# Top-32 cross-attention in a four-layer network: who normalises the first groups, where the keys are made, and where the statistics stand

## The chip, the cores and the metric

The kernel runs on one core of a Trainium2 chip. The core has a TensorE (PE) for matrix products, a VectorE (DVE), a ScalarE (ACT) and a GpSimd (POOL) for elementwise work, and a SyncE (SP) that issues DMAs. The engines run their own instruction streams and wait for each other by semaphores. The metric is the device time of one execution in microseconds.

## What is computed

The network has four layers, each a cross-attention and a feed-forward part, on x of 32 x 128 x 128 (batch, token, feature) in float32. The part that matters here is the attention of layer 1. Its scores keep only the 32 largest of 128 in each row, and its result sets a scale and a shift ("film") on a normalised x:

```
Q = (x_text @ Wq).reshape(Bb, Tt, H, DH)
K = (x_vision @ Wk).reshape(Bb, Gg, H, DH)
scores = jnp.einsum('bthd,bghd->bhtg', Q, K) / np.sqrt(DH).astype(np.float32)
topv, topi = jax.lax.top_k(scores, K_TOP)
probs = jax.nn.softmax(topv, axis=-1)
attn = jnp.zeros_like(scores).at[bi, hi, ti, topi].set(probs)
attn_mean = attn.mean(axis=1)
c_t = jnp.einsum('btg,bgd->btd', attn_mean, V)
x = layernorm(x_text, g_norm_in, b_norm_in)
scale_in, shift_in = jnp.split(c_t @ W_film_in + b_film_in, 2, axis=-1)
x = x * (1.0 + mod_gate * scale_in) + mod_gate * shift_in
y = s4d(x, log_dt, A_re, A_im, C_re, C_im, D_skip)
```

H is 4, DH 32, K_TOP 32. x_text is itself the layernorm of the running x, so x is normalised twice.

## The kernel before

The program is a row of stages with a barrier of all engines between them: stage_front (layer 0 and preparations), stage_film, stage_mix, stage_attention16, stage_fp8, stage_moe, store. stage_film consists of film_in, which is changed, and convolve, which is not. X lies in SBUF as k.X for the whole program.

film_in treats 32 samples i, one a 128 x 128 tile. Four samples are a group g (8 groups), two are a pair (16 pairs). Every engine runs one written-out loop over a pass number p from -5 to 18, and the source order within the loop is the order of its queue. Nothing reorders it. In pass p:

- DVE (from L1408): the statistics of group (p+5)/2 in odd p (group_stats L97: four BN_STATS; group_moments L178 to L188: seven small instructions), the second rstd of group (p+3)/2 in odd p (three small instructions, L1422 to L1427), then four rounds for pair p. A round is 8 MAX8 (L1441, the 8 largest of 128 in each row, 4 heads of 2 samples) and 8 MATCH_REPLACE8 (L1447, takes them out). After four rounds the 32 largest are gone from c_left.
- POOL: c_shift of pair p (L1251, minus the largest, a bias of the exp); in even p rstd of group (p+4)/2 by a pow (L1257) and its normalisation into c_xn (L1262, four instructions); in even p the second rstd and the scaled copy of group (p+2)/2 (L1271 to L1279, three instructions of 128 x 512); the shares of pair p-1 (L1283 to L1293); the film of pair p-2 (L1299, L1301).
- PE: transposes of the weights of pair p-2 (L1315), the scores of pair p+1 (L1325, L1328), in odd p the transposes of c_xn of group (p+3)/2 (L1336), in even p the key product K (L1342, from k.cT, which is there from the start) and the query product Q (L1344) of group (p+2)/2, then for pair p-2 the products L1349 and L1353.
- ACT: exp of what is left of pair p-1 (L1366, c_exb), exp of the scores of pair p (L1373, c_exa), copies of scores (L1380, c_sc), in odd p of c_xnT (L1386), in even p of c_kT (L1392) and c_qT (L1394), then c_wT (L1397), c_aT (L1400) and c_fo (L1406). The difference of the two exps is the softmax over the 32 largest.

A pass is called odd or even by its p. Groups 3 to 7 have their transposes in passes 3, 5, 7, 9 and 11 and K and Q in passes 4, 6, 8, 10 and 12. Rows of q, k and xT share two banks of PSUM: K writes bank 7, the transposes and Q write bank 6.

Of the kernel before, what the change touches and what calls it, by code (L numbers as in the profile page):

```python
# [16 lines left out]
G = 4  # L17
W = G * S
# [1145 lines left out]
def film_in(nc, w, ps, k):  # L1164
# [6 lines left out]
    PAIRS, GROUPS = B // 2, B // G  # L1171
    FIRST, LAST = -5, PAIRS + 3
    TAKES = 2 * H * ROUNDS
    with ExitStack() as ctx:
        def tmp(name, shape, dt=F32):
            return ctx.enter_context(nc.sbuf_tensor("c_" + name, shape, dt))
# [36 lines left out]
        def pair(p):  # L1213
            return (2 * p, 2 * p + 1) if 0 <= p < PAIRS else ()
# [19 lines left out]
        def _(pool):  # L1234
# [10 lines left out]
            for p in range(FIRST, LAST):  # L1245
                for i in pair(p):

                    pool.wait_ge(top_done, TAKES * p + H * (i % 2 + 1))
                    if i >= 4:
                        pool.wait_ge(exb_done, H * (i - 3))  # L1250
                    pool.tensor_scalar(shift[:, i % 4, :], first[:, i % 2, :, 0], -SCALE, None,  # L1251
                                       ALU.mult).then_inc(shift_done, 1)
                if (p + 4) % 2 == 0 and 0 <= (p + 4) // 2 < GROUPS:
                    g = (p + 4) // 2
                    u = g % 2
                    pool.wait_ge(ve, g + 1)
                    pool.tensor_tensor(nm.rstd[:, u], nm.ve[:, u], k.half[:, 0:G], ALU.pow).then_inc(rstd, 1)  # L1257
                    pool.wait_ge(rstd, g + 1)
                    if g >= 4:
                        pool.wait_ge(x3_done, G * (g - 3))  # L1260
                    for j in range(G):
                        pool.tensor_scalar(xn[:, g % 4, j, :], k.X[:, G * g + j, :], nm.mean[:, u, j:j + 1],  # L1262
                                           nm.rstd[:, u, j:j + 1], ALU.subtract, ALU.mult).then_inc(xn_done, 1)
                    pool.tensor_copy(k.mean1[:, G * g:G * g + G], nm.mean[:, u]).then_inc(kept, 1)
                    pool.tensor_copy(k.rstd1[:, G * g:G * g + G], nm.rstd[:, u]).then_inc(kept, 1)
                if (p + 2) % 2 == 0 and 0 <= (p + 2) // 2 < GROUPS:
                    g = (p + 2) // 2
                    u = g % 2
                    x2 = xn[:, g % 4]
                    pool.wait_ge(ve2, g + 1)  # L1270
                    pool.tensor_tensor(rstd2[:, u], rstd2[:, u], k.half[:, 0:G], ALU.pow).then_inc(rstd2_done, 1)  # L1271
                    pool.wait_ge(rstd2_done, g + 1)
                    pool.wait_ge(xT_ps, g + 1)
                    pool.tensor_tensor(x2, x2, rstd2[:, u].rearrange("p (j o) -> p j o", o=1)
                                       .broadcast_to([128, G, 128]), ALU.mult).then_inc(x2a, 1)
                    pool.wait_ge(x2a, g + 1)
                    pool.tensor_tensor(x2, x2, rows(k.gin1), ALU.mult).then_inc(x2b, 1)
                    pool.wait_ge(x2b, g + 1)
                    pool.tensor_tensor(x2, x2, rows(k.bin1), ALU.add).then_inc(x2c, 1)  # L1279
                for i in pair(p - 1):  # L1280
                    a = i % 2
                    pool.wait_ge(exb_done, H * (i + 1))
                    pool.tensor_tensor(share[:, a, :], tota[:, i % 4, :], totb[:, a, :],  # L1283
                                       ALU.subtract).then_inc(tot_done, 1)
                    pool.tensor_tensor(exa[:, i % 4], exa[:, i % 4], exb[:, a], ALU.subtract).then_inc(diff_done, 1)
                    pool.wait_ge(tot_done, i + 1)
                    pool.tensor_tensor(share[:, a, :], share[:, a, :], minus[:], ALU.pow).then_inc(inv_done, 1)
                    pool.wait_ge(inv_done, i + 1)
                    pool.tensor_tensor(share[:, a, :], share[:, a, :], tshare[:, i:i + 1].broadcast_to([128, H]),
                                       ALU.mult).then_inc(share_done, 1)  # L1290
                    pool.wait_ge(share_done, i + 1)
                    pool.wait_ge(diff_done, i + 1)
                    pool.tensor_tensor(exa[:, i % 4], exa[:, i % 4], share[:, a, :].rearrange("p (h o) -> p h o", o=1)  # L1293
                                       .broadcast_to([128, H, 128]), ALU.mult).then_inc(part_done, 1)
                for i in pair(p - 2):
                    x2, f = xn[:, (i // G) % 4, i % G, :], fo[:, i % 2, :]
                    pool.wait_ge(fo_done, i + 1)
                    pool.wait_ge(x2c, i // G + 1)
                    pool.tensor_tensor(x2, x2, f[:, 0:128], ALU.mult).then_inc(filmed, 1)  # L1299
                    pool.wait_ge(filmed, i + 1)  # L1300
                    pool.tensor_tensor(k.x3[:, :, i:i + 1], x2.rearrange("p (c o) -> p c o", o=1),  # L1301
                                       f[:, 128:256].rearrange("p (c o) -> p c o", o=1), ALU.add).then_inc(x3_done, 1)

        @block.tensor
        def _(pe):
            pe.wait_ge(consts, 3)
            pe.wait_ge(zero_aT, 1)
            for p in range(FIRST, LAST):
# [20 lines left out]
                    m.then_inc(sc_ps, 1)  # L1329
                if (p + 3) % 2 == 0 and 0 <= (p + 3) // 2 < GROUPS:  # L1330
                    g = (p + 3) // 2
                    pe.wait_ge(xn_done, G * (g + 1))
                    if g:
                        pe.wait_ge(qT_done, g)
                    for j in range(G):
                        m = pe.transpose(ps[:, 6, j * S:j * S + S], xn[:, g % 4, j, :], k.ident[:])  # L1336
                    m.then_inc(xT_ps, 1)
                if (p + 2) % 2 == 0 and 0 <= (p + 2) // 2 < GROUPS:
                    g = (p + 2) // 2
                    if g:  # L1340
                        pe.wait_ge(kT_done, g)
                    pe.matmul(ps[:, 7, :], k.wk1[:], k.cT[:, W * g:W * g + W], start=True, stop=True).then_inc(k_ps, 1)  # L1342
                    pe.wait_ge(xT_done, g + 1)
                    pe.matmul(ps[:, 6, :], k.wq1[:], xnT[:], start=True, stop=True).then_inc(q_ps, 1)  # L1344
                for i in pair(p - 2):
# [10 lines left out]
        def _(act):  # L1356
            act.wait_ge(consts, 3)
            act.wait_ge(zero_aT, 1)
            for p in range(FIRST, LAST):
# [20 lines left out]
                    act.activation(sc[:, i % 4], ps[:, 0:H, 0:128], ACT.Identity).then_inc(sc_done, 1)  # L1380
                if (p + 3) % 2 == 0 and 0 <= (p + 3) // 2 < GROUPS:
                    g = (p + 3) // 2
                    act.wait_ge(xT_ps, g + 1)
                    if g:
                        act.wait_ge(q_ps, g)
                    act.activation(xnT[:], ps[:, 6, :], ACT.Identity).then_inc(xT_done, 1)  # L1386
                if (p + 2) % 2 == 0 and 0 <= (p + 2) // 2 < GROUPS:
                    g = (p + 2) // 2
                    if g >= 2:
                        act.wait_ge(sc_ps, G * (g - 1))  # L1390
                    act.wait_ge(k_ps, g + 1)
                    act.activation(kT[:, g % 2, :], ps[:, 7, :], ACT.Identity).then_inc(kT_done, 1)  # L1392
                    act.wait_ge(q_ps, g + 1)
                    act.activation(qT[:, g % 2, :], ps[:, 6, :], ACT.Identity).then_inc(qT_done, 1)  # L1394
                for i in pair(p - 2):
# [11 lines left out]

        @block.vector  # L1408
        def _(dve):
            for p in range(FIRST, LAST):  # L1410
                if (p + 5) % 2 == 0 and 0 <= (p + 5) // 2 < GROUPS:
                    g = (p + 5) // 2
                    if g >= 2:
                        dve.wait_ge(kept, 2 * (g - 1))
                        dve.wait_ge(rstd2_done, g - 1)
                    group_stats(dve, nm, norm, g % 2, lambda u, j: k.X[:, G * g + j, :])
                    group_moments(dve, nm, norm, g // 2, g % 2)
                if (p + 3) % 2 == 0 and 0 <= (p + 3) // 2 < GROUPS:
                    g = (p + 3) // 2
                    u = g % 2  # L1420
                    dve.wait_ge(rstd, g + 1)
                    dve.tensor_tensor(rstd2[:, u], nm.rstd[:, u], nm.rstd[:, u], ALU.mult).then_inc(rr, 1)  # L1422
                    dve.wait_ge(rr, g + 1)
                    dve.scalar_tensor_tensor(out=rstd2[:, u], in0=nm.ve[:, u], scalar=EPS, in1=rstd2[:, u],
                                             op0=ALU.subtract, op1=ALU.mult).then_inc(vr, 1)
                    dve.wait_ge(vr, g + 1)
                    dve.tensor_scalar(rstd2[:, u], rstd2[:, u], EPS, None, ALU.add).then_inc(ve2, 1)  # L1427
                for r in range(ROUNDS if pair(p) else 0):
                    done = TAKES * p + 2 * H * r
                    for i in pair(p):  # L1430
                        a = i % 2
# [1467 lines left out]
```

## Time and profile before

| | us |
|---|---|
| median of 3 runs | 1556.45 (1553.75 to 1558.42) |
| profiled execution, time | 1556.44 |
| profiled execution, span | 1554.5 |
| film_in within the span | 218 to 505 |

The span runs from the first to the last recorded instruction. Busy time over the span: PE 77%, DVE 65%, ACT 44%, POOL 38%. These are means over stages of different kinds; in film_in DVE is busy for nearly all the time, and at the end of the program PE is. A row of the timeline gives the start of an instruction or of several alike, its length, engine, line, output and inputs, and in brackets how long its engine had been idle and who released it. L12 is line 12 of the kernel before.

### The profile page before, as it was taken

Reading aid. Unit: us, or ns where it says so; the run is one execution under the profiler, and the core shown is the slowest. Engines: PE = TensorE matmul, PEld = TensorE weight load, DVE = VectorE, ACT = ScalarE, POOL = GpSimd, SP = SyncE. Lnnn points to the kernel's source line nnn. Section 1 sums busy time; section 2 is a strip of 40 time slices with the busy share of each in tenths; the row PEclk is TensorE's granted clock in tenths of the full one; section 3 lists DMA queues with packets and bytes.
Section 4 is the critical chain, followed back from the end, with each engine's and each line's share of the span. In section 5 each row is a group of like instructions: output and inputs, shape, how many; then the busy total and the mean of one; then the engine's idle time right before and its main releaser. Section 6 shows DMA issues by size and latency. Waiting matters only on the chain. (4 is left out here: it accounts for less than half of the span.)

```text
span 1554.5 us, 30934 instructions
## 1 busy us (share of the span) xinstructions
PE 1201.6 (77%) x10597; PEld 813.4 (52%) x10597; DVE 1010.5 (65%) x3921; ACT 685.5 (44%) x1990; POOL 585.7 (38%) x792
## 2 busy tenths in 40 slices
PE   3676743676666678884799897489999969999997
PEld 3443322343443445553577676146666647777765
DVE  6876649999994379852577776557766544444432
ACT  3343335556565344320344443146666633433332
POOL 3466665888876155421222321223333310000000
PEclk8588865666667789996899999589999979898988
DMA  6310041000000511000000000000000000000001
GB/s 164 83 41 1 0 106 26 15 18 28 25 22 28 150 41 42 15 14 14 2 3 3 3 3 3 1 1 1 2 1 2 1 1 1 0 0 0 0 0 54
DMA packets 63678, 35.54 MB, mean 23 GB/s; under 512 B 23925, under 2 KB 61424, under 8 KB 63538
## 3 DMA queue, kind: packets, MB, share of 16 engines
q1 hardware_dynamic: 62234, 33.45, 8.0%
q8 instruction: 76, 1.25, 0.3%
q14 instruction: 64, 0.52, 0.1%
q10 hardware_dynamic: 1304, 0.33, 0.1%
HBM read 25.21 MB, written 6.42 MB: 20 GB/s over the span
## 5 line engine op out<-in xcount | busy, mean ns | idle before, releaser
L2774 DVE SCALAR_TENSOR_TENSOR k_X<-ps,m_gt,k_X 128x128 f32 (+1 forms) x256 | 72.1, 344 | 125.4 <-PE ps L2673 125.4
L2703 ACT ACTIVATE m_hid<-ps,k_b 128x512 f32<-128x512 f32 x128 | 81.8, 684 | 137.5 <-PE ps L2673 127.7
L2673 PEld LDWEIGHTS ps<-k_w,m_hid 128*128 128x128 f32 x1024 | 123.1, 192 | 26.8 <-issue 17.2
L2664 PE MATMUL ps<-m_xnT,k_w 128*128 128x512 f32 x256 | 130.5, 641 | 1.1 <-DVE m_lg L2719 1.1
L2673 PE MATMUL ps<-k_w,m_hid 128*128 128x128 f32 x1024 | 123.4, 275 | 0.0
L2380 POOL TENSOR_TENSOR l_p<-l_p,l_rsum 128x512 f32<-128x512 f32 x64 | 65.2, 1039 | 152.5 <-DVE l_rsum L2611 152.5
L2182 DVE TENSOR_REDUCE g_top<-ps 128x8 f32<-128x1024 f32 x64 | 75.4, 1220 | 50.5 <-PE ps L2050 50.5
L1447 DVE MATCH_REPLACE8 c_left<-c_top,c_left 128x128 f32<-128x128 f32 x384 | 100.9, 276 | 0.0
L2492 ACT ACTIVATE l_p<-ps,l_shift 128x128 f32<-128x128 f32 x256 | 91.3, 387 | 20.2 <-DVE l_shift L2549 20.2
L2130 ACT ACTIVATE g_pT<-ps 128x1024 f32<-128x1024 f32 x64 | 62.0, 1021 | 85.4 <-PE ps L2066 85.4
L692 PE MATMUL ps<-f_expT,f_xeT 128*128 128x512 f32 x128 | 71.0, 686 | 33.6 <-DVE k_X L1064 33.6
L1325 PE MATMUL ps<-c_kT,c_qT 32*128 32x128 f32 x256 | 22.3, 429 | 74.4 <-ACT c_sc L1380 73.1
L1441 DVE MAX8 c_top<-c_left 128x8 f32<-128x128 f32 x384 | 78.6, 277 | 0.0
L121 POOL TENSOR_TENSOR m_rstd<-m_ve,k_half 128x8 f32<-128x8 f32 x4 | 6.6, 1638 | 185.9 <-DVE m_ve L114 185.9
L822 ACT ACTIVATE f_part<-ps,f_wf 128x128 f32<-128x128 f32 x128 | 36.5, 369 | 89.4 <-issue 66.2
L2664 PEld LDWEIGHTS ps<-m_xnT,k_w 128*128 128x128 f32 x256 | 48.6, 208 | 42.6 <-issue 41.1
L692 PEld LDWEIGHTS ps<-f_expT,f_xeT 128*128 128x128 f32 x128 | 25.2, 219 | 67.2 <-DVE k_X L1064 47.9
L1064 DVE SCALAR_TENSOR_TENSOR k_X<-ps,f_wf,k_X 128x128 f32<-128x128 f32 x128 | 44.5, 350 | 24.0 <-PE ps L692 20.6
L1315 PEld LDWEIGHTS ps<-k_ident,c_exa 128*128 128x128 f32 x256 | 45.6, 266 | 25.5 <-POOL c_exa L1293 13.1
L1325 PEld LDWEIGHTS ps<-c_kT,c_qT 32*128 32x128 f32 x256 | 14.5, 260 | 83.8 <-issue 78.2
L2492 ACT ACTIVATION_READ_ACCUMULATOR l_p<-ps,l_shift 128x1 f32 x256 | 58.3, 228 | 0.0
L1353 PE MATMUL ps<-k_wfilm,c_aT 97*128 97x512 f32 x64 | 54.0, 991 | 0.4
(515 smaller groups left out, 3250.2 us busy)
## 6 DMA issues: line engine op xcount, KB each, us to landing
v_toep<-kpad SPq DMA_DIRECT2D x4, 1024.0 KB, 10.4
fo_dram<-c_fo SPq DMA_DIRECT2D x32, 128.0 KB, 1.7
v_late<-kpad SPq DMA_DIRECT2D x4, 1024.0 KB, 10.5
d_fo<-fo_dram SPq DMA_DIRECT2D x8, 512.0 KB, 3.5
k_X<-in_x SPq DMA_DIRECT2D x8, 256.0 KB, 3.5
out<-k_X SPq DMA_DIRECT2D x4, 512.0 KB, 5.4
f_cx<-in_ctx SPq DMA_DIRECT2D x4, 384.0 KB, 5.3
c_cx<-in_ctx SPq DMA_DIRECT2D x4, 384.0 KB, 3.6
```

The lines of the kernel that those rows point to most:

```text
L692: pe.matmul(ps[:, 4 + (2 * b + h) % 3, :], xeT[:, t % 2, u, cols], expT[:, 4 * h:4 * h + 4, :].rearrange("p e d -> p (e d)"), start=True, ...
L1353: pe.matmul(ps[:, 4 + a, :], aT[:, a, :], k.wfilm[:], start=True, stop=True).then_inc(film_ps, 1)
L1441: dve.max((first if r == 0 else top)[:, a, h, :], (sc if r == 0 else left)[:, i % 4, h, :]).then_inc(top_done, 1)
L1447: dve.match_replace(left[:, i % 4, h, :], (first if r == 0 else top)[:, a, h, :], (sc if r == 0 else left)[:, i % 4, h, :], TAKEN).then_in ...
L2130: act.activation(pT[:, n % 2, 2 * h:2 * h + 2, :].rearrange("p a n -> p (a n)"), ps[:, 4 + 2 * h:6 + 2 * h, :].rearrange("p a n -> p (a n) ...
L2182: dve.tensor_reduce(top[:, (n + 1) % 2, :].rearrange("p (r c) -> p r c", r=R)[:, 2 * h:2 * h + 2, 0:R], ps[:, 2 * h:2 * h + 2, :].rearrang ...
L2380: pool.tensor_tensor(p[:, n % 3, 4 * a:4 * a + 4, :], p[:, n % 3, 4 * a:4 * a + 4, :], rsum[:, n % 3, 4 * a:4 * a + 4].rearrange("p (h o) ...
L2492: act.activation(p[:, i % 3, h, :], ps[:, 2 * (i % 2) + a, 128 * b:128 * b + 128], ACT.Exp, bias=shift[:, i % 2, h:h + 1], scale=SCALE, ac ...
L2664: pe.matmul(ps[:, 4 * u + q, :], k.w1_3[:, e, 128 * q:128 * q + 128], xnT[:, u], start=True, stop=True).then_inc(s["hid_ps"].sem, 1)
L2673: m = pe.matmul(ps[:, 4 * u + 2 + e % 2, j * S:j * S + S], hid[:, u, q, j * S:j * S + S], k.w2_3[:, e, q, :], start=q == 0, stop=q == 1)
L2703: act.activation(hid[:, u, q, :], ps[:, 4 * u + q, :], ACT.Gelu, bias=k.b1_3[:, 2 * e + q:2 * e + q + 1]).then_inc(s["hid"].sem, 1)
L2774: dve.scalar_tensor_tensor(out=xj[u][j], in0=ps[:, 4 * u + 2 + e % 2, j * S:j * S + S], scalar=gt[:, u, j, e:e + 1], in1=xj[u][j], op0=ALU ...
```

## The change

DVE's loop is rewritten. It begins with the statistics of groups 0 and 1, then normalises both into c_xn itself (apply), each followed by its second rstd (second). POOL leaves these eight instructions out. Then it loops over the pairs only: the statistics of the next group (moments) stand behind the first round of pair 0 and of odd pairs, the second rstd of group 2 behind the third round of pair 0, and that of later groups ahead of an odd pair. PE makes K in odd passes, ahead of the transposes, in place of even passes ahead of Q, and ACT copies c_kT there, ahead of c_xnT.

```diff
+    EARLY_GROUPS = 2
@@ gpsimd
-                    for j in range(G):
+                    for j in range(G if g >= EARLY_GROUPS else 0):
                         pool.tensor_scalar(xn[:, g % 4, j, :], k.X[:, G * g + j, :], nm.mean[:, u, j:j + 1],
                                            nm.rstd[:, u, j:j + 1], ALU.subtract, ALU.mult).then_inc(xn_done, 1)
@@ tensor
                 if (p + 3) % 2 == 0 and 0 <= (p + 3) // 2 < GROUPS:
                     g = (p + 3) // 2
+                    if g:
+                        pe.wait_ge(kT_done, g)
+                    pe.matmul(ps[:, 7, :], k.wk1[:], k.cT[:, W * g:W * g + W], start=True, stop=True).then_inc(k_ps, 1)
                     pe.wait_ge(xn_done, G * (g + 1))
...
                 if (p + 2) % 2 == 0 and 0 <= (p + 2) // 2 < GROUPS:
                     g = (p + 2) // 2
-                    if g:
-                        pe.wait_ge(kT_done, g)
-                    pe.matmul(ps[:, 7, :], k.wk1[:], k.cT[:, W * g:W * g + W], start=True, stop=True).then_inc(k_ps, 1)
@@ scalar
                     g = (p + 3) // 2
+                    if g >= 2:
+                        act.wait_ge(sc_ps, G * (g - 1))
+                    act.wait_ge(k_ps, g + 1)
+                    act.activation(kT[:, g % 2, :], ps[:, 7, :], ACT.Identity).then_inc(kT_done, 1)
                     act.wait_ge(xT_ps, g + 1)
...
                     g = (p + 2) // 2
-                    if g >= 2:
-                        act.wait_ge(sc_ps, G * (g - 1))
-                    act.wait_ge(k_ps, g + 1)
-                    act.activation(kT[:, g % 2, :], ps[:, 7, :], ACT.Identity).then_inc(kT_done, 1)
@@ vector
+            def apply(g):
+                u = g % 2
+                dve.wait_ge(rstd, g + 1)
+                dve.wait_ge(mean, g + 1)
+                for j in range(G):
+                    dve.tensor_scalar(xn[:, g % 4, j, :], k.X[:, G * g + j, :], nm.mean[:, u, j:j + 1],
+                                      nm.rstd[:, u, j:j + 1], ALU.subtract, ALU.mult).then_inc(xn_done, 1)
...
+            moments(0)
+            moments(1)
+            for g in range(EARLY_GROUPS):
+                apply(g)
+                second(g)
+            for p in range(PAIRS):
+                if p % 2 == 1 and (p + 3) // 2 >= 3 and (p + 3) // 2 < GROUPS:
+                    second((p + 3) // 2)
+                for r in range(ROUNDS):
+                    if r == 1 and (p == 0 or p % 2 == 1) and (p + 5) // 2 < GROUPS:
+                        moments((p + 5) // 2)
+                    if r == 3 and p == 0:
+                        second(2)
```

moments and second hold the same instructions and waits as before. In the order of instructions this looks as follows. ACT, from the scores' copies of an odd pass to c_wT of the next even one (c_ names are tiles of film_in, ps is PSUM), before:

```order
L1380 ACTIVATE c_sc<-ps 128x512 x2
L1386 ACTIVATE c_xnT<-ps 128x512
L1397 ACTIVATE c_wT<-ps 128x128 x2
L1400 ACTIVATE c_aT<-ps 96x128 x2
L1406 ACTIVATE c_fo<-ps 128x512 x2
L1366 ACTIVATE c_exb,c_totb<-c_left,c_shift 128x128 x8
L1373 ACTIVATE c_exa,c_tota<-c_sc,c_shift 128x128 x8
L1380 ACTIVATE c_sc<-ps 128x512 x2
L1392 ACTIVATE c_kT<-ps 128x512
L1394 ACTIVATE c_qT<-ps 128x512
L1397 ACTIVATE c_wT<-ps 128x128 x2
```

And the same stretch of ACT in the changed kernel:

```order
L1381 ACTIVATE c_sc<-ps 128x512 x2
L1387 ACTIVATE c_kT<-ps 128x512
L1391 ACTIVATE c_xnT<-ps 128x512
L1398 ACTIVATE c_wT<-ps 128x128 x2
L1401 ACTIVATE c_aT<-ps 96x128 x2
L1407 ACTIVATE c_fo<-ps 128x512 x2
L1367 ACTIVATE c_exb,c_totb<-c_left,c_shift 128x128 x8
L1374 ACTIVATE c_exa,c_tota<-c_sc,c_shift 128x128 x8
L1381 ACTIVATE c_sc<-ps 128x512 x2
L1395 ACTIVATE c_qT<-ps 128x512
L1398 ACTIVATE c_wT<-ps 128x128 x2
```

The copy of c_kT moved from the even pass to the odd one, where it stands ahead of c_xnT and so of the pair's c_wT, c_aT and c_fo. On PE the odd pass has these rows in the changed kernel, from the scores to the film products:

```order
L1326 MATMUL ps<-c_kT,c_qT 128x128 x4
L1329 MATMUL ps<-k_vmask,c_onesb 128x128 x4
L1335 MATMUL ps<-k_cT,k_wk 128x512
L1340 MATMUL ps<-k_ident,c_xn 128x128 x4
L1350 MATMUL ps<-c_wT,c_cx 96x128 x2
L1354 MATMUL ps<-k_wfilm,c_aT 128x512 x2
```

The row L1335, the key product, is new in this place; the transposes L1340 followed the scores directly before. On DVE the opening, behind the statistics of group 1, differs so (- before, + changed):

```order
 L188 TENSOR_SCALAR c_ve<-c_m 128x4
-L1422 TENSOR_TENSOR c_rstd<-c_rstd 128x4
-L1424 SCALAR_TENSOR_TENSOR c_rstd<-c_ve,c_rstd 128x4
-L1427 TENSOR_SCALAR c_rstd<-c_rstd 128x4
+L1423 TENSOR_SCALAR c_xn<-k_X,c_mean,c_rstd 128x128 x4
+L1430 TENSOR_TENSOR c_rstd<-c_rstd 128x4
+L1432 SCALAR_TENSOR_TENSOR c_rstd<-c_ve,c_rstd 128x4
+L1435 TENSOR_SCALAR c_rstd<-c_rstd 128x4
```

The three instructions of the second rstd now have the four of the normalisation ahead of them; four rows alike follow for group 1, and then the first round of pair 0, before the statistics of group 2.

## Rows read from the trace of the kernel before

**Rows 1.** The page: the span.
```profile
span 1554.5 us, 30934 instructions
```

**Rows 2.** Timeline of the opening: start, length (us), engine, line, idle before it.
```profile
221.77 0.23 DVE L188 TENSOR_SCALAR c_ve<-c_m 128x4 f32<-128x4 f32 x1
224.82 1.09 PE L1336 MATMUL ps<-k_ident,c_xn 128*128 128x128 f32 x4 [17.32 <-POOL c_xn L1262]
229.36 0.60 ACT L1394 ACTIVATE c_qT<-ps 128x512 f32<-128x512 f32 x1 [1.11 <-PE ps L1344]
231.59 1.26 POOL L1277 TENSOR_TENSOR c_xn<-c_xn,k_gin 128x512 f32<-128x512 f32 x1
231.76 1.12 DVE L182 TENSOR_TENSOR c_d<-c_diff 128x4 f32<-128x4 f32 x1
232.66 0.60 ACT L1380 ACTIVATE c_sc<-ps 128x512 f32<-128x512 f32 x1 [1.10 <-PE ps L1328]
234.61 1.64 DVE L1441 MAX8 c_first<-c_sc 128x8 f32<-128x128 f32 x8
```

**Rows 3.** Timeline of DVE: statistics ahead of pair 1, then its first maxima.
```profile
249.15 0.86 DVE L97 BATCH_NORM_STATS2 c_stats<-k_X 128x6 f32<-128x128 f32 x4
...
251.32 1.64 DVE L1441 MAX8 c_first<-c_sc 128x8 f32<-128x128 f32 x8
```

**Rows 4.** Timeline of DVE in a later stage: eight normalisations of one tile.
```profile
1269.89 2.14 DVE L130 TENSOR_SCALAR m_xn<-k_X,m_mean,m_rstd 128x128 f32<-128x128 f32 x8 [1.82 <-POOL m_rstd L121]
```

**Rows 5.** Timeline: ACT's exp of the last pair, DVE's first instruction in convolve.
```profile
487.42 0.39 ACT L1366 ACTIVATE c_exb<-c_left,c_shift 128x128 f32<-128x128 f32 x1
...
517.78 0.69 DVE L1507 COPY k_x<-ps 128x512 f32<-128x512 f32 x1 [33.53 <-PE ps L1488]
```

**Rows 6.** Timeline of ACT from odd pass 5 to odd pass 7.
```profile
330.82 0.60 ACT L1406 ACTIVATE c_fo<-ps 128x512 f32<-128x512 f32 x1 [1.11 <-PE ps L1353]
...
339.15 0.60 ACT L1380 ACTIVATE c_sc<-ps 128x512 f32<-128x512 f32 x1 [1.10 <-PE ps L1328]
...
341.21 0.60 ACT L1392 ACTIVATE c_kT<-ps 128x512 f32<-128x512 f32 x1 [1.47 <-PE ps L1342]
342.86 0.60 ACT L1394 ACTIVATE c_qT<-ps 128x512 f32<-128x512 f32 x1 [1.05 <-PE ps L1344]
...
352.17 0.39 ACT L1373 ACTIVATE c_exa<-c_sc,c_shift 128x128 f32<-128x128 f32 x1
...
356.93 0.60 ACT L1380 ACTIVATE c_sc<-ps 128x512 f32<-128x512 f32 x1 [1.10 <-PE ps L1328]
357.97 0.60 ACT L1386 ACTIVATE c_xnT<-ps 128x512 f32<-128x512 f32 x1 [0.45 <-PE ps L1336]
...
363.71 0.60 ACT L1406 ACTIVATE c_fo<-ps 128x512 f32<-128x512 f32 x1 [1.11 <-PE ps L1353]
```

**Rows 7.** Timeline of POOL and ACT: what starts the exps of an odd pass.
```profile
266.81 0.23 POOL L1251 TENSOR_SCALAR c_shift<-c_first 128x4 f32<-128x4 f32 x1 [6.01 <-DVE c_first L1441]
...
298.29 0.60 ACT L1406 ACTIVATE c_fo<-ps 128x512 f32<-128x512 f32 x1 [1.11 <-PE ps L1353]
...
319.27 0.40 ACT L1373 ACTIVATE c_exa<-c_sc,c_shift 128x128 f32<-128x128 f32 x1 [2.11 <-POOL c_shift L1251]
...
351.53 0.44 POOL L1251 TENSOR_SCALAR c_shift<-c_first 128x4 f32<-128x4 f32 x2
...
448.54 0.41 POOL L1251 TENSOR_SCALAR c_shift<-c_first 128x4 f32<-128x4 f32 x2
...
450.49 0.39 ACT L1373 ACTIVATE c_exa<-c_sc,c_shift 128x128 f32<-128x128 f32 x1
```

**Rows 8.** Timeline of ACT: the second film copy of pass 4.
```profile
313.50 0.60 ACT L1406 ACTIVATE c_fo<-ps 128x512 f32<-128x512 f32 x1 [0.26 <-PE ps L1353]
```

**Rows 9.** By stretch: length, busy PE, PEld, DVE, ACT, POOL, granted clock, DMA; passes 7, 4.
```profile
354.00:363.50 9.50, 6.67 (x25) 3.60 (x26) 9.50 (x64) 4.50 (x16) 5.93 (x10) 0.50 0.01 4
309.50:314.00 4.50, 3.50 (x14) 1.70 (x14) 4.46 (x29) 2.53 (x8) 4.34 (x8) 1.00 0.00 0
```

More of the change, by code:

```diff
@@ L1409, in _ @@
         def _(dve):
[L1410 to L1428, printed above, removed]
@@ new lines, in moments @@
+            def moments(g):
+                if g >= 2:
+                    dve.wait_ge(kept, 2 * (g - 1))
+                    dve.wait_ge(rstd2_done, g - 1)
+                group_stats(dve, nm, norm, g % 2, lambda u, j: k.X[:, G * g + j, :])
+                group_moments(dve, nm, norm, g // 2, g % 2)
+            def apply(g):
[5 more added lines that the diff above has]
+                                      nm.rstd[:, u, j:j + 1], ALU.subtract, ALU.mult).then_inc(xn_done, 1)
@@ new lines, in second @@
+            def second(g):
+                u = g % 2
+                dve.wait_ge(rstd, g + 1)
+                dve.tensor_tensor(rstd2[:, u], nm.rstd[:, u], nm.rstd[:, u], ALU.mult).then_inc(rr, 1)
+                dve.wait_ge(rr, g + 1)
+                dve.scalar_tensor_tensor(out=rstd2[:, u], in0=nm.ve[:, u], scalar=EPS, in1=rstd2[:, u],
+                                         op0=ALU.subtract, op1=ALU.mult).then_inc(vr, 1)
+                dve.wait_ge(vr, g + 1)
+                dve.tensor_scalar(rstd2[:, u], rstd2[:, u], EPS, None, ALU.add).then_inc(ve2, 1)
```

## The prediction

> **What bounds the kernel now.** I read the page first, then the timeline of the stage film_in (218 to 505 us) on each engine, then who released whom at the start and the end of a pass. The profiled execution spans 1554.5 us [rows 1] and took 1556.44 us, so 1.9 us lie around the span; the median of the runs is 1556.45, so a sum made against the profiled run carries over unchanged. Of all stages only film_in is touched, and barriers stand around it: what it gains or loses passes whole to the end.
>
> VectorE looks like the bound: from its first MAX8 at 234.61 it works nearly without a pause on the 16 pairs. But read the end. DVE is idle for 33.53 us before 517.78, so its last instruction ended at 484.25, while ACT began the exp of the last pair only at 487.42, right behind its own copies of the pass before [rows 5]. The end of the stage is set by ACT, 3.2 us behind DVE. Following ACT back: its exps of an odd pass start either by its own order (352.17, 450.49: no wait) or are released by POOL's c_shift (319.27, 2.11 us of waiting) [rows 6, 7]. POOL in turn goes without a pause from ACT's last c_fo of an odd pass through the whole even pass to the next odd c_shift. So there is a loop ACT, PE, POOL of two passes, in which DVE has no part. Its halves:
> - odd half, from exa to the second c_fo: 352.17 to 363.71, 11.54 us [rows 6];
> - even half by ACT, from second c_fo to the next odd exa: 330.82 to 352.17, 21.35 us [rows 6]; by POOL: 298.29 to 319.27, 20.98 us [rows 7].
> The longer of the two ends the even half. The last place at which DVE held the loop is pass 2: POOL waited 6.01 us for c_first and wrote c_shift at 266.81 [rows 7]. So the change has two prices: what it does to DVE up to pair 2, and what it does to the loop from pass 3 on.
>
> **Part 1, opening.** DVE normalises group 0 instead of POOL. Eight such instructions took 2.14 us [rows 4], one per 0.26; four end about 1.12 us after they start. They start when the second moments end, at about 221.9 [rows 2], so group 0 is there at 223.0; before, TensorE's transposes began at 224.82, which puts it at 224.7: 1.7 us earlier. The K product no longer stands between transposes and Q product: c_qT was copied at 229.36; a product that has PE for itself is 2.06 from start to copy (339.15 to 341.21, rows 6), which would give 228.7, 0.6 earlier. The second scores, complete at 232.66 + 0.60 = 233.26 [rows 2], are then complete at 231.0. Before, DVE only began its maxima at 234.61, because the statistics of group 2 waited for POOL (c_d took 1.12 us there beside POOL's L1277 [rows 2], and another of the same length follows). The eight maxima of a round took 1.64, so the four of the pair's second sample began about 0.8 later, at 235.4; now they begin when the second scores are there, at 231.0: 4.4 us earlier.
> The statistics of group 2 have not gone: they stand behind the first round of pair 0. Statistics and second rstd together took 2.17 us undisturbed (249.15 to 251.32 [rows 3]), 1.7 of it the statistics. 4.4 less 1.7 leaves 2.7 us for pair 2, if nothing stalls. But the second rstd of group 2 now falls, by POOL's own order of about 10 us from statistics to the end of x2, into POOL's 512-wide products, and the statistics of group 3 into those of pair 0. A DVE instruction with two inputs that met such a product lasted 1.12 us, where the small one of 221.77 took 0.23 [rows 2]. Two such meetings in each of the two places make up to 4 us. From -2.7 to +1.4, I take +0.5, nearer to the meetings, since POOL's products fill most of both windows.
>
> **Part 2, K ahead of the transposes, in odd passes.** For groups 3 to 7, in passes 3, 5, 7, 9 and 11, PE now makes K before the transposes, and ACT copies kT before xnT, both before wT, aT and the film products of the pair. Nothing hides it: ACT waits for PE in that place already. Before, xnT began 1.04 after the second c_sc (356.93 to 357.97). Now kT begins 2.06 after it (as 339.15 to 341.21), the transposes run behind K while kT is copied, and xnT begins 1.04 later, at 3.10: the odd half grows by 2.06 us [rows 6]. Five times: +10.3 us.
>
> **Part 3, even passes.** There only Q is left; c_qT begins where c_kT did, 1.65 us earlier (341.21 for 342.86 [rows 6]). But the even half then ends by POOL. In passes 4 and 10 POOL ended it already (319.27 [rows 7]; pass 10 alike): no gain. In passes 6 and 8 ACT was late by 0.37 (352.17 against 351.53 + 0.27 for the c_shift [rows 6, 7]): 2 x 0.37. In pass 12, without a group for POOL to normalise, POOL was ready at 448.54 and ACT at 450.49 [rows 7]: the whole 1.65. Together -2.4 us. Passes 13 to 16 have no group and stay.
>
> **Part 4, the rest.** DVE's later statistics behind the first round of an odd pair and its own stalls cost nothing at the end: by then the loop is later than DVE and gets still later, so that DVE will wait for scores. Group 1's normalisation on DVE lies ahead of the first scores, and four POOL instructions a group fall away where POOL is idle. No DMA is moved.
>
> **Sum.** +0.5 +10.3 -2.4 = +8.4 us. TensorE was granted half of its clock in pass 7, that is 1.2 GHz, and the whole, 2.4 GHz, while the films of pass 4 ran [rows 9]. There the second copy waited 0.26 us [rows 8], where it waits 1.11 at the low level [rows 6]: 0.85 less. The first copy's wait must fall about as much, some 1.6 us for both (an estimate from these two rows). With K the odd passes are denser, and I allow such a rise in one or two of the five: -1.9. So +6.5 us: **1563.0 us**.
>
> **Rivals.**
> 1. DVE bounds the stage after all (for it: it is busy in nearly all of it; against it: the 3.2 us at the end and the loop that doesn't pass it). Then parts 2 and 3 count nothing, and part 1 alone stands, -2.7 to +1.4: 1553.7 to 1557.8 us, no measurable change. Chance 0.15.
> 2. The clock rises in every odd pass at its film products. Each pass then costs 2.06 - 1.6 = 0.45: 5 x 0.45 - 2.4 + 0.5 = +0.4, 1556.8 us. For it: the same rise in pass 4. Against it: pass 7 of before had none [rows 9], and in pass 6, with K and Q in a row, c_kT waited 1.47 and c_qT 1.05 us [rows 6], too long for the higher level. Chance 0.19.
> 3. The other side: the clock is up from K on in each odd pass. K then costs some 1.0 in place of 2.06 (half, an estimate), and transposes, aT and films give back 2.2 (the 1.6 and a little for the rest): the odd half is 1.2 us shorter than before, 5 x -1.2 - 2.4 + 0.5 = -7.9, 1548.5 us. It decides from the point where the rise comes before the second scores are copied. Chance 0.07; another 0.02 for anything else that is faster.
> The Trainium skill (TensorE: Matmul & The Clock Gate, What's actually happening) says that activity releases a throttle which is otherwise on: by it denser odd passes are granted more clock, which is rivals 2 and 3. The trace agrees in part: the stretch of pass 4 at 1.00 had PE busy for 3.50 of 4.50 us, but pass 7 with 6.67 of 9.50 stayed at 0.50 [rows 9].
>
> **Numbers.** The forecast with its neighbours (slower by over 0.3%, 4.7 us, about what a measurement of this kernel tells from no change) has 0.57, no change 0.34, faster 0.09. The upper bound is the sum with every product at the low clock and all the meetings of part 1 (+9.3) and a little for clock elsewhere: 1567. The lower one takes in rivals 1 and 2, down to 1553.5. The forecast's own range is 1561 to 1566.
>
> **What would show it.** Right: between the first c_fo and exa nothing new; in odd passes c_kT waits about 1.5 us for L1335 and xnT begins some 3.1 us after the second c_sc; the odd half 13.6 in place of 11.5; even halves all near 20.98 and released by POOL; DVE with idle time before the maxima of pairs 6 to 15, waiting for c_sc; its first MAX8 near 229.3, POOL's c_shift of pair 2 between 264 and 268; ACT's last exb near 494. Wrong: if the odd half is under 12.5 us (rivals 2, 3), if DVE never waits and ACT's last exb is released by c_left (rival 1), or if c_shift of pair 2 lies outside that stretch (part 1).

## The result

The changed kernel takes 1564.53 us (median of 8 runs, 1560.74 to 1567.16) where the kernel before takes 1556.95 in the same comparison: a ratio of 1.005, with an interval of 1.0036 to 1.0064. It is slower by half a per cent. The profiled execution took 1560.74 us and spans 1558.7.

```profile
span 1558.7 us, 30936 instructions
PE 1208.1 (78%) x10597; PEld 817.9 (52%) x10597; DVE 1019.4 (65%) x3929; ACT 685.4 (44%) x1990; POOL 579.3 (37%) x784
```

The counts on the page show what was moved: 8 instructions more on DVE, 8 fewer on POOL. They say nothing of the time. The 9 us that DVE is busier are mostly not the 8 instructions (about 2 us) but small ones that were held up.

One execution's span says little, either, because the stage ahead of the changed one ends at times several us apart: film_in's first DVE instruction stands at 218.40 us in the trace of before, at 215.88 in that of after, and anywhere from 215.4 to 222.5 over all twelve traces of this document. So from here on times of the stage are counted **from that instruction**. So counted they agree between kernels to hundredths wherever nothing was changed. Three marks are used: DVE's first MAX8, POOL's c_shift of pair 2, and the start of ACT's exp of the last pair.

| mark, us from the stage's start | before | after |
|---|---|---|
| DVE's first MAX8 | 16.21 | 10.77 |
| c_shift of pair 2 | 48.41 | 49.04 |
| ACT's exp of the last pair | 269.02 | 275.89 |

The opening does begin 5.4 us earlier. Two pairs later all of it is gone, and at the end 6.9 us are lost. Behind film_in nothing changed: from ACT's first copy in convolve (507.53 and 511.77) to the end of the span it is 1047.0 us before and 1046.9 after.

The opening in the timeline of DVE and POOL in the changed kernel, answering [rows 2] and the first row of [rows 7]:

```profile
226.65 0.87 DVE L1462 MAX8 c_first<-c_sc 128x8 f32<-128x128 f32 x4 [3.45 <-ACT c_sc L1381]
228.35 0.87 DVE L1462 MAX8 c_first<-c_sc 128x8 f32<-128x128 f32 x4 [0.82 <-ACT c_sc L1381]
...
264.92 0.23 POOL L1252 TENSOR_SCALAR c_shift<-c_first 128x4 f32<-128x4 f32 x1 [9.43 <-DVE c_first L1462]
```

DVE waits for the scores, as it should, and no longer for POOL. POOL waits 9.43 us for pair 2's first maxima, where it waited 6.01: it is ready for them earlier than before, and DVE is not.

The odd pass 3 on ACT, answering the lower half of [rows 6]:

```profile
289.60 0.60 ACT L1381 ACTIVATE c_sc<-ps 128x512 f32<-128x512 f32 x1 [1.10 <-PE ps L1329]
291.67 0.60 ACT L1387 ACTIVATE c_kT<-ps 128x512 f32<-128x512 f32 x1 [1.47 <-PE ps L1335]
292.46 0.60 ACT L1391 ACTIVATE c_xnT<-ps 128x512 f32<-128x512 f32 x1 [0.20 <-PE ps L1340]
...
296.49 0.60 ACT L1407 ACTIVATE c_fo<-ps 128x512 f32<-128x512 f32 x1 [1.74 <-PE ps L1354]
298.19 0.60 ACT L1407 ACTIVATE c_fo<-ps 128x512 f32<-128x512 f32 x1 [1.11 <-PE ps L1354]
```

c_xnT begins 2.86 us after the second c_sc, where it began 1.04 after it. ACT waits 1.47 for K, copies it, and only then gets the transposes. The loop's next two links, in the timeline of ACT: the exps of passes 5 and 7 with the end of the odd pass between them.

```profile
319.17 0.40 ACT L1374 ACTIVATE c_exa<-c_sc,c_shift 128x128 f32<-128x128 f32 x1 [1.24 <-POOL c_shift L1252]
...
332.53 0.60 ACT L1407 ACTIVATE c_fo<-ps 128x512 f32<-128x512 f32 x1 [1.11 <-PE ps L1354]
...
353.53 0.40 ACT L1374 ACTIVATE c_exa<-c_sc,c_shift 128x128 f32<-128x128 f32 x1 [1.68 <-POOL c_shift L1252]
...
491.77 0.39 ACT L1367 ACTIVATE c_exb<-c_left,c_shift 128x128 f32<-128x128 f32 x1
```

The odd half is 332.53 - 319.17 = 13.36 us (11.55 before), the even half 353.53 - 332.53 = 21.00 and ended by POOL. Over all passes the halves read off in this way are:

| | odd 3, 5, 7, 9, 11 | even 4, 6, 8, 10, 12 |
|---|---|---|
| before | 11.54 to 11.55 | 20.98, 21.35, 21.35, 20.98, 21.35 |
| after | 13.35 to 13.37 | 20.98, 21.00, 20.98, 20.97, 19.64 |

The ledger closes: +0.63 at c_shift of pair 2, +9.05 in five odd halves, -2.44 in the even ones, -0.36 in pass 14, where ACT's wait before the second c_sc was 0.74 in place of 1.10. That makes +6.88; measured is +6.87.

### The profile page after: what moved, and what is told of

The parts are those of the page before. It is cut to its first block and busy times, and to the rows that moved or that the text cites. A ratio compares the mean times of both kernels' runs of the same rounds, so it can differ in the third digit from the quotient of the medians.

```text
span 1558.7 us, 30936 instructions
## 1 busy us (share of the span) xinstructions
PE 1208.1 (78%) x10597; PEld 817.9 (52%) x10597; DVE 1019.4 (65%) x3929; ACT 685.4 (44%) x1990; POOL 579.3 (37%) x784
## 3 DMA queue, kind: packets, MB, share of 16 engines
q8 instruction: 76, 1.25, 0.3%
## 5 line engine op out<-in xcount | busy, mean ns | idle before, releaser
L2685 PE MATMUL ps<-m_xnT,k_w 128*128 128x512 f32 x256 | 127.3, 628 | 1.1 <-DVE m_lg L2740 1.1
L1316 PE MATMUL ps<-k_ident,c_exa 128*128 128x128 f32 x256 | 49.6, 367 | 9.6 <-POOL c_exa L1294 9.6
```

What stands on the lines that cost most here:

```text
L1316: m = pe.matmul(ps[:, 4 + a, 0:128], exa[:, i % 4, h, :], k.ident[:], start=h == 0, stop=h == H - 1)
L2685: pe.matmul(ps[:, 4 * u + q, :], k.w1_3[:, e, 128 * q:128 * q + 128], xnT[:, u], start=True, stop=True).then_inc(s["hid_ps"].sem, 1)
```

## The experiments

Theory: ACT, PE and POOL form a loop that ends the stage, and K in the odd passes lengthened it. Rivals: DVE's new order cost the time; or TensorE's clock answers to the denser passes and decides. All times of the stage are from its start, as above.

**K in even passes again (e1).** Only group 0 keeps its K ahead of the transposes.

```diff
+                    if g == 0:
                         pe.matmul(ps[:, 7, :], k.wk1[:], ...)      # odd pass, and ACT's copy alike
...
+                    if g > 0:
+                        pe.matmul(ps[:, 7, :], k.wk1[:], ...)      # even pass, and ACT's copy alike
```

> The changed kernel with K made and copied in even passes again for groups 1 to 7; only group 0 keeps it ahead of the transposes. Loop theory (ACT, PE and POOL end the stage; the copy of K in odd passes lengthened it): odd halves go back from 13.35 to 11.54 us, even halves end at 20.98 to 21.35; ACT's last c_exb starts 269.6 us after the stage's first DVE instruction (275.9 in the changed kernel, 269.0 before); time about 6.3 us under the changed kernel, 1557.5, no difference from before. Rival (DVE's statistics behind the first round cost it): stays at 275.9 and 1564.

Measured: 1560.2 us beside 1554.22, ratio 1.0039 (1.0024 to 1.0053); the last exp at 273.59. The odd halves went back to 11.54 to 11.55, as expected. The total did not: the even halves rose to 22.13 to 22.16, over anything that POOL or ACT need (here and below, even halves are those of passes 4 to 10; in pass 12 POOL has no group to normalise). POOL's row at the start of even pass 6 tells why:

```profile
337.91 0.46 POOL L1302 TENSOR_TENSOR k_x<-c_xn,c_fo 128x128 f32<-128x128 f32 x1
338.92 0.23 POOL L1252 TENSOR_SCALAR c_shift<-c_first 128x4 f32<-128x4 f32 x1 [0.55 <-DVE c_first L1473]
339.69 0.22 POOL L1252 TENSOR_SCALAR c_shift<-c_first 128x4 f32<-128x4 f32 x1 [0.54 <-DVE c_first L1473]
```

POOL waits for DVE's maxima there; in the trace of before both c_shift of that pass run in one piece without a wait. So with the K move undone the stage is bound by DVE, and DVE is slower than before. This miss is the most useful of the runs: the change has **two** costs, and in the changed kernel one hides the other.

**K moved alone (e2).** The kernel before with K and its copy in odd passes.

```diff
@@ tensor, scalar: odd pass
+                    pe.matmul(ps[:, 7, :], k.wk1[:], ...)
...
@@ tensor, scalar: even pass
-                    pe.matmul(ps[:, 7, :], k.wk1[:], ...)
```

> The kernel before with K and its copy moved to odd passes, nothing else. Loop theory: odd halves 13.35 us, pair 2's c_shift as before, ACT's last c_exb at 269.0 + 5 x 1.8 - 2.4 = 275.6 us from the stage's start; time about 6.5 us over before, 1563.5. Rival (DVE's new order cost it): 269.0 and 1557.

Measured: 1563.27 us, ratio 1.005 (1.0033 to 1.0066); the last exp at 275.33; odd halves 13.36 to 13.37; c_shift of pair 2 at 48.42. The loop theory's number was 275.6. K alone gives 6.3 of the 6.9 us. Its c_kT and c_xnT stand in the odd pass as in the changed kernel:

```profile
290.01 0.60 ACT L1380 ACTIVATE c_sc<-ps 128x512 f32<-128x512 f32 x1 [1.10 <-PE ps L1328]
292.07 0.60 ACT L1386 ACTIVATE c_kT<-ps 128x512 f32<-128x512 f32 x1 [1.46 <-PE ps L1334]
292.87 0.60 ACT L1390 ACTIVATE c_xnT<-ps 128x512 f32<-128x512 f32 x1 [0.20 <-PE ps L1339]
```

**K made twice (e7).**

```diff
+                    if g >= 3:
+                        pe.matmul(ps[:, 7, :], k.wk1[:], k.cT[:, W * g:W * g + W], start=True, stop=True)
                     pe.matmul(ps[:, 7, :], k.wk1[:], k.cT[:, W * g:W * g + W], start=True, stop=True).then_inc(k_ps, 1)
```

> The changed kernel with the K product made twice in odd passes 3 to 11. Loop theory: each odd half grows by one more product at the low clock, about 1.9 us, so ACT's last c_exb is 9.5 us later than in the changed kernel, 285.4 us from the stage's start, time about 1574. Clock rival (a denser odd pass is granted the higher clock): the odd half grows by under 1 us or shrinks, at most 1569. DVE rival: no change, 1564.5.

Measured: 1565.91 us, ratio 1.0064 (1.004 to 1.0087); the last exp at 282.87, 7.0 us after the changed kernel's (9.5 were expected). Passes 3, 5, 7 and 9 took 15.06 to 15.07, 1.71 more each for one product. Pass 11 took 12.98, less than with one K. In that pass the clock rose, and the timeline of ACT shows where:

```profile
440.60 0.60 ACT L1389 ACTIVATE c_kT<-ps 128x512 f32<-128x512 f32 x1 [3.17 <-PE ps L1337]
441.38 0.60 ACT L1393 ACTIVATE c_xnT<-ps 128x512 f32<-128x512 f32 x1 [0.19 <-PE ps L1342]
...
444.18 0.60 ACT L1409 ACTIVATE c_fo<-ps 128x512 f32<-128x512 f32 x1 [1.00 <-PE ps L1356]
445.04 0.60 ACT L1409 ACTIVATE c_fo<-ps 128x512 f32<-128x512 f32 x1 [0.26 <-PE ps L1356]
```

The two c_fo waited 1.00 and 0.26 us in place of 1.74 and 1.11. The stretch from 440 to 452 has a granted clock of 0.93 in this run. So both held: the product is on the loop, and the higher clock does come in such a pass, once in five at this density and not at all at the changed kernel's.

**More work for DVE (e8).**

```diff
+                    if r == 2 and 3 <= p <= 11:
+                        for j in range(2):
+                            dve.bn_stats(spare[:, j], k.X[:, j, :])
```

> The changed kernel with 2 more BN_STATS on DVE in each of pairs 3 to 11, into a spare tile that nobody reads: 18 x 0.217 = 3.9 us of DVE's time. Loop theory: DVE's waits ahead of pairs 13 to 15 shrink and ACT's last c_exb stays at 275.9 us from the stage's start within 0.4. DVE rival: 279.8.

Measured in one execution: the last exp at 276.19, 0.3 us later for 3.9 us of work; DVE's last instruction of the stage ended at 274.90 in place of 273.07, still ahead of it, and DVE's waits ahead of pairs 13 and 14 are gone. Even the 0.3 us are not DVE's: they are pass 14's wait before the second c_sc, 1.10 in place of 0.74, and e6 and e7 show the same 1.10 without the added work. POOL never waits for DVE from pass 3 on. Those waits are here, in the changed kernel:

```profile
442.81 0.87 DVE L1462 MAX8 c_first<-c_sc 128x8 f32<-128x128 f32 x4 [1.16 <-ACT c_sc L1381]
444.51 0.87 DVE L1462 MAX8 c_first<-c_sc 128x8 f32<-128x128 f32 x4 [0.83 <-ACT c_sc L1381]
458.88 0.87 DVE L1462 MAX8 c_first<-c_sc 128x8 f32<-128x128 f32 x4 [0.52 <-ACT c_sc L1381]
```

DVE is not the bound of the changed kernel. It had at least the 3.9 us to spare; how much more, no run tests.

**K out of the loop (e3).** K is made in the odd pass, but behind the film products, where PE waits for ACT; it is copied in the even pass.

```diff
                     pe.matmul(ps[:, 4 + a, :], aT[:, a, :], k.wfilm[:], start=True, stop=True).then_inc(film_ps, 1)
+                if (p + 3) % 2 == 0 and 1 <= (p + 3) // 2 < GROUPS:
+                    g = (p + 3) // 2
+                    pe.wait_ge(kT_done, g)
+                    pe.matmul(ps[:, 7, :], k.wk1[:], k.cT[:, W * g:W * g + W], start=True, stop=True).then_inc(k_ps, 1)
```

> The changed kernel with K of groups 1 to 7 made behind the film products of the odd pass, where PE waits for ACT anyway, and copied in the even pass ahead of c_qT. Loop theory: odd halves 11.54 us, ACT's even half 1.65 shorter than before and so ended by POOL at 20.98; ACT's last c_exb at 269.0 + 0.6 - 2.4 = 267.2 us from the stage's start, time about 1555. If K delays the transposes or scores of the next pass: 269 to 271.

Measured: 1556.19 us beside 1554.05, ratio 1.0024 (1.0004 to 1.0044); the last exp at 271.80, odd halves 11.53 to 11.55, even ones 22.14 to 22.17. The odd half is as expected, and 2.4 us were to come from the even ones, which DVE now holds as in e1. DVE's last instruction ends at 271.95, behind the start of ACT's last exps.

**The second cost: where the statistics stand (e4, e5).** e4 is e3 with group 2's second rstd and group 3's statistics at the start of pair 1, where POOL is idle. e5 goes on: all later statistics at the start of odd pairs, as in the kernel before.

```diff
@@ e4
+                if p == 1:
+                    moments(3)
-                if p % 2 == 1 and (p + 3) // 2 >= 3 and (p + 3) // 2 < GROUPS:
+                if p % 2 == 1 and (p + 3) // 2 < GROUPS:
                     second((p + 3) // 2)
...
-                    if r == 1 and (p == 0 or p % 2 == 1) and (p + 5) // 2 < GROUPS:
+                    if r == 1 and (p == 0 or p % 2 == 1 and p > 1) and (p + 5) // 2 < GROUPS:
@@ e5
-                if p == 1:
-                    moments(3)
+                if p % 2 == 1 and (p + 5) // 2 < GROUPS:
+                    moments((p + 5) // 2)
...
+                    if r == 1 and p == 0:
+                        moments(2)
```

> e3 with second(2) and moments(3) at the start of pair 1, where POOL has nothing to do, in place of behind rounds of pairs 0 and 1. If the stalls of DVE beside POOL's products took the opening's gain: pair 2's c_shift comes 3.7 us earlier than in the changed kernel (45.4 us from the stage's start, 49.0 there, 48.4 before), and ACT's last c_exb at 263.5 us, time about 1551.5. If DVE, with its later stalls, is then the bound, it is 264 to 267. Rival (the place makes no difference): 49.0 and as e3.

> e4 with all later statistics at the start of odd pairs, as in the kernel before; only those of group 2 stand behind the first round of pair 0. Loop theory: the same as e4 as long as ACT and POOL end the stage (263.5 us); where DVE has become the bound in e4, its stalls fall from about 8 to about 5 us and this one is up to 3 us faster than e4. Rival (later statistics behind the first round are worth having): slower than e4.

Measured for e4: 1553.48 us, ratio 1.0004 (0.9983 to 1.0024); c_shift of pair 2 at 45.63, 3.4 us earlier than in the changed kernel; the last exp at 267.92; even halves still 22.13 to 22.15. For e5: **1548.76 us, ratio 0.996 (0.9944 to 0.9976)**, faster than both kernels; the last exp at 262.82, even halves 20.99 to 21.00. Between e4 and e5 the same instructions stand in other places, and 5.1 us lie between them. Both expectations had that cost too low: with DVE as the bound e4 was to end at 264 to 267, and e5 at most 3 us ahead of it. The timeline of DVE shows both at the same group. First e4, at the start of pair 5 and behind its first round, with one row of POOL that is used further down:

```profile
308.60 0.49 DVE L1441 TENSOR_TENSOR c_rstd<-c_rstd 128x4 f32<-128x4 f32 x1
309.13 0.16 DVE L1443 SCALAR_TENSOR_TENSOR c_rstd<-c_ve,c_rstd 128x4 f32<-128x4 f32 x1
309.32 1.16 DVE L1446 TENSOR_SCALAR c_rstd<-c_rstd 128x4 f32<-128x4 f32 x1
...
315.29 1.27 DVE L182 TENSOR_TENSOR c_d<-c_diff 128x4 f32<-128x4 f32 x1
...
309.18 1.27 POOL L1286 TENSOR_TENSOR c_exa<-c_exa,c_exb 128x512 f32<-128x512 f32 x1
```

Then e5, both together at the start:

```profile
307.76 0.19 DVE L178 TENSOR_TENSOR c_diff<-c_stats 128x4 f32<-128x4 f32 x1
307.88 0.15 DVE L179 TENSOR_TENSOR c_m<-c_stats 128x4 f32<-128x4 f32 x1
307.95 1.25 DVE L180 TENSOR_TENSOR c_mean<-c_stats 128x4 f32<-128x4 f32 x1
309.23 0.16 DVE L182 TENSOR_TENSOR c_d<-c_diff 128x4 f32<-128x4 f32 x1
```

In two places the small instructions of this group are held three times (0.49, 1.16, 1.27, together 2.4 us over their 0.16); in one place once (1.25, 1.1 over). Two pairs of DVE cost 31.25 us without any of it: 2 x 14.54 for the rounds (265.86 - 251.32 in the trace of before) and 2.17 [rows 3]. With 2.4 it is 33.7, just what e1, e3 and e4 show as sum of the two halves (11.55 + 22.15). With 1.1 it is 32.35, under the loop's 11.55 + 20.99 = 32.54. Once a group is not a rule, though. In pair 9 of e5 two instructions are held (0.39 and 1.19), and in pair 9 of e2, where all stands in one place too, three (0.50, 1.16, 1.16). It depends on what POOL is doing at that moment.

What holds them is seen when POOL's rows are laid beside DVE's, in the changed kernel:

```profile
285.17 1.28 DVE L182 TENSOR_TENSOR c_d<-c_diff 128x4 f32<-128x4 f32 x1
286.37 0.16 DVE L183 TENSOR_SCALAR c_mean<-c_mean 128x4 f32<-128x4 f32 x1
286.48 0.16 DVE L185 SCALAR_TENSOR_TENSOR c_m<-c_d,c_m 128x4 f32<-128x4 f32 x1
...
285.16 1.26 POOL L1286 TENSOR_TENSOR c_exa<-c_exa,c_exb 128x512 f32<-128x512 f32 x1
286.38 1.03 POOL L1288 TENSOR_TENSOR c_share<-c_share,c_minus 128x4 f32<-128x4 f32 x1
```

A product on POOL begins at 285.16; a DVE instruction of 4 columns begins at 285.17 and ends with it, at 286.45 and 286.42. The Trainium skill (SBUF — State Buffer, Who interferes with whom) says that a DVE instruction with two inputs in SBUF and a GpSimd instruction that reads SBUF block each other for the whole instruction, and that the one issued later waits. That is what these rows show. They also show its limit: the pow of L1288, with both inputs in SBUF, runs for 1.03 us, and DVE's two-input instruction at 286.48 is not held.

One such pair of rows could be chance. Over the twelve traces, 161 of the small instructions in film_in took more than 0.3 us, and every one of them ended between 0.01 and 0.03 us after a product, sum or difference of POOL on two tiles (1.04 to 1.28 us long, or 0.46 on 128 columns) that had started first or at the same moment. Of the 161, 61 are a TENSOR_SCALAR with a single input, as the one at 309.32 in e4: it ended at 310.48, POOL's L1286 at 310.45. So in these traces it is not only two-input instructions that are held. And where no such product runs, nothing is held: with the statistics of group 3 at the start of pair 1 (e4) the 3.5 us of holding in pairs 0 and 1 fall to 0.1.

**POOL normalises again (e6).**

```diff
-    EARLY_GROUPS = 2
+    EARLY_GROUPS = 0
```

> The changed kernel, but POOL normalises groups 0 and 1 as before. By the sum of the opening: DVE's first maxima 1.7 us later than the changed kernel's 10.8 us from the stage's start, so 12.5, pair 2's c_shift 50.5 to 50.8 in place of 49.0, and ACT's last c_exb 277.5 in place of 275.9. Rival (the first scores hang on something else): no change.

Measured in one execution: DVE's first MAX8 at 12.47 (10.77 with DVE's norms), c_shift of pair 2 at 50.75 (49.04), the last exp at 277.99 (275.89). The 1.7 us of the opening are as expected, and at pair 2 they are 1.7 still. Of the 2.1 us at the last exp the other 0.4 are the wait of pass 14 again.

**K in odd passes with good statistics (e9).** The changed kernel with the statistics placed as in e5.

```diff
+                if p % 2 == 1 and (p + 5) // 2 < GROUPS:
+                    moments((p + 5) // 2)
-                    if r == 1 and (p == 0 or p % 2 == 1) and (p + 5) // 2 < GROUPS:
-                        moments((p + 5) // 2)
+                    if r == 1 and p == 0:
+                        moments(2)
```

> The changed kernel (K in odd passes for all groups) with the statistics of groups 3 to 7 and all second rstds at the start of odd pairs as before; only group 2's statistics behind the first round of pair 0. Loop theory: with K in odd passes the loop is longer than DVE's two pairs wherever the statistics stand, so only the opening counts: pair 2's c_shift at 45.6 us from the stage's start (49.0 in the changed kernel) and ACT's last c_exb 3.4 us before the changed kernel's 275.9, so 272.5; time about 1558 beside 1554 of before. If the statistics' place costs by itself, as between e4 and e5: 5 us more than that, 267.4.

Measured: the last exp at 272.53, exactly the loop theory's 272.5; odd halves 13.35 to 13.36. With K in the odd passes the place of the statistics counts for nothing but the opening: 3.4 us, the gain at c_shift of pair 2 (45.64 for 49.04). The time is 1562.8 beside 1554.49, ratio 1.0053 (1.0034 to 1.0073), so 5 to 11 us over the kernel before (1558 was expected), while the stage in its trace is only 3.5 us longer and the rest of the span as long as before. What the unprofiled runs lose beyond that is open: where the stage begins and what follows it are not on record for them.

**Statistics in POOL's pause (e10).** e5 with those of pairs 3 to 11 ahead of the fourth round.

```diff
+                    if r == 3 and p % 2 == 1 and p > 1:
+                        if (p + 5) // 2 < GROUPS:
+                            moments((p + 5) // 2)
+                        if (p + 3) // 2 < GROUPS:
+                            second((p + 3) // 2)
```

> e5 with the statistics and second rstds of odd pairs from 3 on placed ahead of the fourth round, where POOL waits 2.8 us for c_fo. If POOL's two-input products are what stretches DVE's small instructions: those of 0.25 us and more lose most of the 5.7 us that they exceed 0.16 by in e5, and DVE's last instruction ends 2 to 4 us earlier than 262.6 from the stage's start. The end then hangs on the loop alone, so ACT's last c_exb stays near 262.8 (262.0 to 262.8). If the stretch has another cause: 5 us or more of it remain.

Measured: 1551.2 us, ratio 0.9968 (0.9953 to 0.9982); the last exp at 263.32, DVE's last instruction ends at 261.43 (262.56 in e5). The pause was missed: in pair 5 c_diff was held for 1.20 us at 318.51, while POOL's pause lay between 322.06 and 324.88. Of the 5.7 us of holding 4.7 remain, which is neither of the two cases expected. So this run says nothing on whether the pause helps. In pair 3 the ten small instructions stood from 287.26 to 288.64, most of them within a pow of POOL (287.11 to 288.11), and none was held. The time is no better than e5's.

| | last exp, from stage start | time over before, us |
|---|---|---|
| before | 269.0 | |
| changed | 275.9 | +7.6 |
| K moved alone (e2) | 275.3 | +9.1 |
| DVE's order alone, nearly (e1) | 273.6 | +6.0 |
| K late (e3) | 271.8 | +2.1 |
| and pair 1 clean (e4) | 267.9 | -0.6 |
| and statistics as before (e5) | 262.8 | -5.3 |

Taken as differences to before, the two columns agree within 1.4 us except for e2, where the time lost 2.7 us more than the stage. The last column is a difference of two medians, and the traces' own spans are not it: in that of e5 the part of the program behind film_in took 4 to 5 us longer than in the others (1051.4 us from ACT's first copy in convolve, elsewhere 1046.8 to 1047.7).

## Why the prediction was right, and where it was not

1563.0 us was forecast and 1564.5 measured. The bound was read rightly, from the end of the stage and not from DVE's busy share. By its steps:

- **Opening.** DVE's first MAX8 was expected at about 10.9 us from the stage's start (229.3 less 218.4) and came at 10.77; c_shift of pair 2 was to be 0.5 later than before and was 0.63. The four meetings with POOL were there: 0.91 and 1.12 us in the second rstd of group 2 (240.20 and 241.34), 0.89 and 1.15 in the statistics of group 3 (250.88 and 252.01).
- **Odd halves.** The term was 2.06 a pass and measured 1.81: c_xnT followed c_kT after 0.79, not 1.04. The 1.04 had been read where the transposes began 0.11 us before the second c_sc (356.82 for 356.93 in the trace of before). Behind K they took as long, 1.06 us for 1.11, but began 0.31 us before c_kT (291.36 for 291.67). Five passes: 1.25 us too much.
- **Even halves.** -2.4 was forecast, -2.44 measured, pass by pass as told.
- **The clock.** 1.9 us were allowed for a rise in one or two odd passes. It came in none: c_fo waited 1.74 and 1.11 us in each of the five, and this busy stretch of pass 3 stayed at the lower of the two levels.

```profile
292.00:298.00 6.00, 5.15 (x11) 2.34 (x11) 6.00 (x43) 2.34 (x7) 1.32 (x3) 0.50 0.01 4
```

  That is the row by stretch from 292 to 298 us: length, busy PE, PEld, DVE, ACT, POOL, granted clock. PE is busy for 5.15 of 6 us at 0.50. The two errors have opposite signs and nearly cancel, 1.25 against 1.9; that the sum came out is partly luck. Nothing came of rival 2, which had 0.19.
- **Passes 13 to 16** were to stay. Pass 14 was 0.36 us shorter, from the wait before its second c_sc. That does not follow from the new order: the clock granted in the 2 us before that copy was 0.99 in the trace of after and 0.50 in that of before, and e6, e7 and e8, whose ACT and PE keep the changed order, show the 1.10 of before.
- **Part 4 failed in one point.** DVE's later statistics were called free "since the loop is later than DVE". In the changed kernel this holds (e8, e9). But the step overlooked that they are a cost of their own of nearly the same size: e1, with the loop mended, is still 4.6 us long in the stage. And DVE waited only for pairs 13 and 14, not from pair 6 on: its two pairs took 32.5 to 33.7 us, not 31.25.
- **Rival 1**, DVE as the bound at no change in time, was wrong on both counts. The stage changed, and where DVE does become the bound (e1, e3, e4) it costs time.

## What to carry to other kernels

An engine that is busy all the time need not be the bound: look at which engine does the last thing of a stage, go back from there, and write down the loop with its halves. A product moved to an engine's idle time must stand where the waiting engine is not next in line; here the same K costs 1.8 us a pass ahead of the transposes and nothing behind the films. And when two costs run side by side, undoing one shows only the difference to the other: undo both, one after the other, before judging either.

## What the runs showed of the hardware

- Small instructions of VectorE with 4 columns take 0.16 us alone and up to 1.28 beside a two-input product of GpSimd on 512 columns, ending with it, with one input as well as with two. MAX8 and MATCH_REPLACE8 beside the same products keep their 0.28 us. A pow of GpSimd on 4 columns, 1.03 us long, holds nobody up. Spread over two places of a pair, the ten instructions were held three times in each group of e4; together in one place once to twice a group in e5, but up to three times in e2.
- PE at half clock can stay there with 5.15 of 6 us busy, and in another run with 1.7 us more of products in the pass rise in one pass of five.
